# Modulation computed as rows with the weights streamed, and loads in another order, in an AdaLN block on one core

## The reference

```python
mod = (_silu(L0_c) @ L0_wmod).reshape(2, 6, 1, 512)      # L0_c (2, 512), L0_wmod (512, 3072)
sa, ca, ga, sb, cb, gb = (mod[:, 0], ..., mod[:, 5])
ga = (2 * (ga >= 0) - 1) * jnp.maximum(jnp.abs(ga), 0.25)   # gb likewise
h = _layernorm(x) * (1 + ca) + sa
x = x + ga * attn(h)      # projection 512x512, rotation of 64 features, relu, tanh, group norm,
                          # then swapaxes and reshape (tokens and channels change places)
h = _layernorm(x) * (1 + cb) + sb
x = x + gb * ffn(h)       # gate, up (512 -> 1376), silu(gate) * up, down; each weight is lut[idx],
                          # a table of 16 values looked up by an int32 index matrix
```

## Time and profile before

| | us |
|---|---|
| median of 3 runs | 1061.77 (1061.48 to 1063.47) |
| the profiled execution: its time | 1063.87 |
| the profiled execution: its span | 1061.6 |
| start, to the first projection | 0 to 46.48 |
| block 0 | 46.48 to 89.75 (43.27) |
| block 1 | 89.75 to 131.02 (41.27) |
| block 2 | 131.02 to 184.04 (53.02) |
| block 3 | 184.04 to 221.26 (37.22) |
| bridge, to the first feed-forward matmul | 221.26 to 266.13 (44.87) |
| the rest | 266.13 to 1061.6 |

### The profile page before, as it was taken

How to read it: one execution, slowest core, us unless ns; L and a number is a source line. 1 busy time by engine, 2 the same in 40 slices (tenths; PEclk the granted TensorE clock), 3 DMA queues, 4 the chain that set the end, 5 groups by cost and what they waited for, 6 DMA issues and landing times.

```text
span 1061.6 us, 13109 instructions
## 1 busy us (share of the span) xinstructions
PE 960.3 (90%) x4480; PEld 464.8 (44%) x4480; DVE 603.0 (57%) x1384; ACT 410.0 (39%) x621; POOL 185.2 (17%) x156
## 2 busy tenths in 40 slices
PE   5869669977888988999899999999999999999998
PEld 5534326433333433444444444444444444444443
DVE  5599995997589874334887876322222432222312
ACT  2365854566554633224543532332222421222200
POOL 3111202036456540112202200110000101000000
PEclk9989887988899999999999999999999999999999
DMA  8667363531001021234235114222000112000011
GB/s 291 214 178 218 68 185 64 178 100 40 20 20 30 20 80 50 80 110 119 40 119 158 32 48 159 80 70 89 0 0 0 55 44 102 0 0 0 1 40 40
DMA packets 33740, 83.40 MB, mean 79 GB/s; under 512 B 2977, under 2 KB 2977, under 8 KB 30625
## 3 DMA queue, kind: packets, MB, share of 16 engines
q1 hardware_dynamic: 32544, 74.47, 21.4%
q0 software_dynamic: 1152, 8.39, 4.3%
HBM read 63.98 MB, written 18.87 MB: 78 GB/s over the span
## 4 chain that ended last, share of the span: by engine, by line
PE 68%; DVE 17%; issue 6%; ACT 5%; DMA 1%; SPq 1%; POOL 1%; DVEq 0%; ACTq 0%; POOLq 0%
PE ps L1163 27%; PE ps L1197 22%; PE ps L1130 7%; PE ps L1152 4%; DVE hid L834 3%; PE ps L1118 2%; DVE R L856 2%; PE ps L1175 2%; PE ps L1210 2%; DMA w_all<-wmod_dram 1%; DVE hd L865 1%; ACT R L571 1%; DVE st L750 1%; ACT w_all L562 1%; PE ps L1142 1%
## 5 line engine op out<-in xcount | busy, mean ns | idle before, releaser
L1163 PE MATMUL ps<-h,w_all 128*128 128x512 f16 x1920 | 424.7, 383 | 18.8 <-DVE hd L865 16.3
L1163 PEld LDWEIGHTS ps<-h,w_all 128*128 (+1 forms) x1920 | 188.5, 99 | 252.3 <-issue 19.5
L1197 PE MATMUL ps<-w_all,hid 128*128 128x512 f16 x1056 | 231.1, 381 | 4.7 <-DVE w_all L1047 4.7
L1197 PEld LDWEIGHTS ps<-w_all,hid 128*128 128x128 f16 x1056 | 103.6, 98 | 129.5 <-DVE w_all L1047 5.2
L865 DVE SCALAR_TENSOR_TENSOR hd<-ps,col,sg 128x512 f32<-128x512 f32 x80 | 59.9, 748 | 149.5 <-ACT sg L532 149.5
L532 ACT ACTIVATE sg<-ps,col 128x512 f32<-128x512 f32 x80 | 54.6, 682 | 181.8 <-PE ps L1163 181.1
L890 DVE SCALAR_TENSOR_TENSOR hd<-ps,col,gbB 128x512 f32<-128x512 f32 x32 | 24.0, 751 | 148.4 <-PE ps L1197 148.1
L1152 PE MATMUL ps<-hid,w_all 128*128 128x512 f16 x352 | 90.1, 419 | 12.9 <-DVE hid L834 12.9
L547 ACT ACTIVATE hid<-hd 128x512 f16<-128x512 f32 (+1 forms) x88 | 55.0, 628 | 113.0 <-DVE hd L865 99.7
L1130 PE MATMUL ps<-WQ,work 128*128 128x512 f16 x384 | 89.1, 394 | 4.0 <-DVE col L980 3.1
L427 POOL TENSOR_TENSOR h<-h,h 128x512 f16<-128x512 f32 x32 | 37.3, 1186 | 306.5 <-ACT h L517 306.5
(11 more groups left out here) (112 smaller groups left out, 840.6 us busy)
## 6 DMA issues: line engine op xcount, KB each, us to landing
R<-x_dram SPq DMA_DIRECT2D x16, 1024.0 KB, 6.9
xa<-x_dram SPq DMA_DIRECT2D x14, 1024.0 KB, 6.2
hid<-idx_dram SPq DMA_DIRECT2D x44, 256.0 KB, 6.9
R<-bias_dram POOLq DMA_DIRECT2D x8, 1024.0 KB, 8.4
out_dram<-R SPq DMA_DIRECT2D x32, 256.0 KB, 2.2
x_dram<-R SPq DMA_DIRECT2D x7, 1024.0 KB, 5.0
w_all<-wmod_dram SPq DMA_DIRECT2D x6, 1024.0 KB, 15.2
h<-idx_dram SPq DMA_DIRECT2D x11, 256.0 KB, 2.6
```

Of the source, the lines that this page charges most:

```text
L1163: ins = nc.tensor.matmul(bank(GU[2 * s + t]), W[wp][:, bass.ds(at, P)], h2[hp][:, s, k], start=(k == 0 and i == 0), stop=(k == K - 1 and i ...
L1197: ins = nc.tensor.matmul(bank(QY[par]), hid[hp][:, bass.ds(at, P)], W[wp][:, w_at:w_at + BLK], start=(j == 0 and i == 0), stop=(j == J - 1 ...
```

## The change

Each section is now one product of 4 matmuls: `cT`, widened to 32 columns (the two batches repeated 16 times), is stationary, and 512 columns of weights stream past. The result is a tile of 32 rows at partitions 0, 32 or 64 of one PSUM bank (`mod_product`). ScalarE copies it to SBUF (`copy_mod`). `mod_vec` then turns rows into vectors by transposes of 2x128 pieces, four for each section; `mod_row` repeats a row over all partitions by one matmul for each batch, with a column of the identity broadcast. The gate is made once on the 32 rows (`gate_rows`), and VectorE only copies the repeated rows out. GA's vectors and rows are made after block 0's projection, and those of SB, CB and GB in block 3 and the bridge. The loop of TensorE over blocks now covers 1 and 2.

```diff
             load_mod(SA)
+            load_x(x_toks[0, 0], 0)
+            load_mod(CA)
             sp.dma_start(wq_f32, wq.rearrange("(k p) n -> p k n", p=P)).then_inc(wq_in, 16)
-            load_mod(CA)
-            load_x(x_toks[0, 0], 0)
             load_idx(0, 0)
-            load_idx(1, 1)
             load_mod(GA)
...
-            load_rows(0, rows_of_block(0, 0))
-            for s in (SB, CB, GB):
-                load_mod(s)
+            load_idx(1, 1)
+            load_x(x_toks[0, 1], 1)
             for w in range(2, AHEAD):
                 load_idx(w, w % 2)
+            load_rows(0, rows_of_block(0, 0))
...
+                if q == 0:
+                    load_idx(AHEAD, 0)
+                    store_bias(0)
+                for w in range(AHEAD * (q + 1) + (q == 0), AHEAD * (q + 2) - last):
                     load_idx(w, w % 2)
+                if q == 0:
+                    for s in (SB, CB, GB):
+                        load_mod(s)
...
+            def copy_mod(n, sections):
+                act.wait_ge(mod_mm, n + 1)
+                for i in (s % 3 for s in sections):
+                    ins = nc.scalar.activation(mod_rows[i], bank(QY[1])[32 * i:32 * (i + 1)], ACT.Copy)
+                ins.then_inc(mod_copied, 1)
+
+            copy_mod(0, (SA, CA))
+            norm(0)
             act.wait_ge(lut_split, 1)
             half_idx(0, 0)
+            act.wait_ge(vec_ready, 1)
+            affine(0, CA, SA, 0, hq[0], lambda: None, halves=(0,))
+            copy_mod(1, (GA,))
+            affine(0, CA, SA, 0, hq[0], lambda: None, halves=(1,))
             half_idx(1, 1)
-            norm(0)
-            act.wait_ge(vec_ready, 1)
-            affine(0, CA, SA, 0, hq[0], lambda: None)
-            act.wait_ge(row_ready, 1)
-            make_bias(0)
...
+                if q == 0:
+                    tanh(q, 3)
+                    act.wait_ge(row_ready, 1)
+                    make_bias(0)
                 if not last:
                     norm(q + 1)
-                tanh(q, 3)
+                if q:
+                    tanh(q, 3)
...
+                    copy_mod(2, (SB, CB, GB))
...
+            stats(0)
             dve.wait_ge(wq_in, 16)
             magnitude(wq_s, wq_f32)
             v.tensor_reduce(c_wqmax, wq_s, axis=AX, op=ALU.max).then_inc(wq_max, 1)
-            stats(0)
...
+            def gate_rows(n):
+
+                dve.wait_ge(mod_copied, n + 1)
+                m = mod_rows[GA]
+                gate_of(m, m, mod_rows[SA], mod_rows[CA]).then_inc(gate_made, 1)
...
-                step(gate_of(flat(vec[:, GA]), flat(gate_ps[:, GA]), gs[:, 3, 0:K * BATCH],
-                             gs[:, 3, K * BATCH:2 * K * BATCH]))
+                v.tensor_copy(vec[:, GA], gate_ps[:, GA])
                 for b in range(BATCH):
                     dve.wait_ge(row_mm, b + 1)
-                    step(gate_of(gaB[:, b], bank(GU[b]), hd[:, 0], hd[:, 1]))
-                    ins = v.memset(col[:, 14:15], 0.0)
+                    ins = v.tensor_copy(gaB[:, b], bank(GU[b]))
                 ins.then_inc(row_ready, 1)
             masks(0, 0)
-            gates_of_attn()
+            gate_rows(1)
...
+                if q == 0:
+                    rope_relu(q, q, 3)
+                    gates_of_attn()
                 if not last:
                     stats(q + 1)
-                rope_relu(q, q, 3)
+                if q:
+                    rope_relu(q, q, 3)
...
-                if q == NB - 2:
-                    scales_of_ffn()
...
             stats(LN_B[0], xa, 1)
+            scales_of_ffn()
+            gate_rows(2)
...
-                step(gate_of(gbB[:, b], bank(QY[b]), hd[:, 0], hd[:, 1]))
+                ins = v.tensor_copy(gbB[:, b], bank(QY[b]))
+            step(ins)
...
+            def mod_product(sections):
+
                 for s in sections:
+                    i = s % 3
                     pe.wait_ge(mod_in[s], 16)
+                    for k in range(K):
+                        ins = nc.tensor.matmul(bank(QY[1])[32 * i:32 * (i + 1)],
+                                               cT[:, k],
+                                               mod_w[s][:, k], start=k == 0, stop=k == K - 1)
+                ins.then_inc(mod_mm, 1)
...
+                        ins = nc.tensor.transpose(bank(to)[:, at:at + BATCH],
+                                                  mod_rows[s % 3][0:BATCH, kb * P:(kb + 1) * P],
+                                                  ident[0:BATCH, 0:BATCH])
...
-            mod_vec((SA, CA))
-            mod_vec((GA,), GU[3])
-            transpose_x(0, 0)
-            mod_row(GA, GU)
+            mod_product((SA, CA))
+            mod_vec(0, (SA, CA))
+            pe.wait_ge(vec_ready, 1)
+            transpose_x(0, 0, halves=(0,))
+            mod_product((GA,))
+            transpose_x(0, 0, halves=(1,))
             pe.wait_ge(wq_ready, 1)
             pe.wait_ge(diag_ready, 1)
+            pe.wait_ge(mod_copied, 2)
...
                 project(q, q, 0)
+                if gates:
+                    pe.wait_ge(gate_made, 1)
+                    mod_vec(1, (GA,), GU[3])
+                    mod_row(GA, GU)
+                    pe.wait_ge(row_ready, 1)
...
                 if last:
-                    mod_row(GB, QY)
+                    pe.wait_ge(q_taken, A * NB)
+                    mod_product((SB, CB, GB))
                     transpose_g(q, q)
...
-                if scales:
-                    mod_vec((SB, CB))
+                if last:
+                    mod_vec(2, (SB, CB))
...
+            pe.wait_ge(vec_ready, 2)
+            mod_row(GB, QY)
             for i in range(3, 6):
                 sum_chunk(w + i, i % 2)
```

More of the change, by code:

```diff
@@ L316, in _ @@
                     load_early_rows()
-                for w in range(AHEAD * (q + 1), AHEAD * (q + 2) - last):
+                if q == 0:
+                    load_idx(AHEAD, 0)
+                    store_bias(0)
+                for w in range(AHEAD * (q + 1) + (q == 0), AHEAD * (q + 2) - last):
                     load_idx(w, w % 2)
+                if q == 0:
+                    for s in (SB, CB, GB):
+                        load_mod(s)
                 if not last:
@@ L1207, in mod_vec @@
+            def mod_vec(n, sections, to=QY[1]):
+                pe.wait_ge(mod_copied, n + 1)
+                for s in sections:
                     for kb in range(K):
                         at = (s * K + kb) * BATCH
-                        for k in range(K):
-                            ins = nc.tensor.matmul(bank(to)[:, at:at + BATCH], mod_w[s][:, k, kb * P:(kb + 1) * P],
-                                                   cT[:, k], start=k == 0, stop=k == K - 1)
+                        ins = nc.tensor.transpose(bank(to)[:, at:at + BATCH],
+                                                  mod_rows[s % 3][0:BATCH, kb * P:(kb + 1) * P],
+                                                  ident[0:BATCH, 0:BATCH])
@@ L1212, in mod_vec @@
                 ins.then_inc(vec_mm, 1)
             def mod_row(s, banks):
-                if banks is QY:
-                    pe.wait_ge(q_taken, A * NB)
-                pe.wait_ge(mod_in[s], 16)
+                pe.wait_ge(gate_made, s // 3 + 1)
                 for b in range(BATCH):
-                    for k in range(K):
-                        ins = nc.tensor.matmul(bank(banks[b]), cT[:, k, b:b + 1].broadcast_to((P, P)),
-                                               mod_w[s][:, k], start=k == 0, stop=k == K - 1)
-                    ins.then_inc(row_mm, 1)
+                    nc.tensor.matmul(bank(banks[b]), ident[0:BATCH, b:b + 1].broadcast_to((BATCH, P)),
+                                     mod_rows[s % 3][0:BATCH], start=True, stop=True) \
+                      .then_inc(row_mm, 1)
@@ L1234, in attn_block @@
+            def attn_block(q, last=False, gates=False):
                 w = AHEAD * q
                 project(q, q, 0)
+                if gates:
[3 more added lines that the diff above has]
+                    pe.wait_ge(row_ready, 1)
                 sum_chunk(w, 0, True)
@@ L1248, in attn_block @@
                     transpose_g(q, q + 1)
-            pe.wait_ge(row_ready, 1)
-            with pe.Fori(0, NB - 2) as q:
+            attn_block(0, gates=True)
+            with pe.Fori(1, NB - 1) as q:
                 attn_block(q)
-            attn_block(NB - 2, scales=True)
-            pe.wait_ge(vec_ready, 2)
             attn_block(NB - 1, last=True)
```

24 lines of the change are left out of this document (10 added, 14 removed).

## The result

| | median us | lowest to highest | runs |
|---|---|---|---|
| before | 1062.0 | 1061.5 to 1066.2 | 10 |
| after | 1056.2 | 1053.5 to 1059.9 | 10 |

The ratio is 0.9942, with an interval from 0.9924 to 0.9959: 5.8 us faster, where 14.4 were forecast. The profiled execution of after took 1054.04 (span 1051.8), that of before 1063.87 (span 1061.6).

A forecast was written before the change was run, and what follows sets the result against it. Start bound by the modulation chain, blocks 0 and 1 by VectorE, block 2 lengthened by `mod_vec` and a slow `sum_chunk`. -11.0 + 1.6 + 5.4 - 11.7 + 0.5 + 0.8 = -14.4, from 1061.8 to 1047.4; range 1041.0 to 1054.0.

The forecast's parts named there:

- Start, 1.1 too much: Start: reordered loads and streamed products bring the first projection from 46.48 to 35.5, a gain of 11.0.
- Rival (c): Start: GpSimd's 5.74 of issue begins only with the maximum, low halves near 33, projection 39.0; +3.5, 1050.9; chance 0.13.
- Block 0, right: Block 0: gate copies behind the fourth `rope_relu` add 1.6 on VectorE, which bounds the block.
- Block 1, 3 too little: Block 1: SB, CB and GB queued ahead of block 2's tokens make VectorE's statistics wait, +5.4, at most 6.4.
- Block 2, right: Block 2: loses `mod_vec` and the slow `sum_chunk`, becoming 41.27 instead of 53.02, -11.7.
- Block 3, 1.2 too little gain: Block 3: three-section product takes 10.5 against `mod_row`'s 7.03, partly regained in the second transposes; +0.5, between 0 and 1.2.
- Bridge, 1.7 too little: Bridge: scales and `gate_rows` delay VectorE by 2.5, mostly covered; +0.8, between 0 and 2.9.
- so this is covered there: Bridge: VectorE's added 2.5 hides in its 5.72 idle for GpSimd's index conversion; if not, it costs the 2.5.
- (a): Block 1: the three megabytes are hidden and there is no wait; 1042.0; chance 0.20.
- (b): Start: streamed products do not bring TensorE's clock up; gain 5.2 instead of 11.0, 1053.2; chance 0.12.
- (d): Start and block 3: products using only 32 output columns sink TensorE to 1.2 GHz; slower, +3.2, 1065.0; chance 0.04.
- (e): Start: reordering does nothing because something else holds the projection near 46; 1058 to 1061; chance 0.03.

The follow-up runs named there:

- each alone: After with GA's product moved behind the second transposes of block 0: 1055.2 us; or after with the maximum across partitions left out: 1053.3 us.
- both 2.9: After with GA's product behind the second transposes and the maximum across partitions left out too: projection at 33.67, 1051.2 us, ratio 0.9872.

## Why the prediction was wrong

Most mechanisms were named rightly, and no rival came out whole. But two covers were assumed that were not there, two sizes were off, and so was the choice of base. The forecast missed by 8.8: 4.6 in the stages, 4.0 in the base, 0.2 in the median of before itself.

- **Start, 1.1 too much.** Loads, products, norm and transposes came as worked out. The step that failed is "the low half at 34.98 started at once after ScalarE, with no such gap": that row had 11.65 of idle ahead of it, which hid GpSimd's way back from its library. Rival (c) had two halves. The first fell, because the 5.93 ended 1.5 after the maximum, not 5.7 later. The second held: 7.29 of issue ahead of the low halves. The low halves began at 30.04, and the projection came 1.1 later than forecast, not 3.5. How much of the 1.1 is this gap's is not shown apart from the other chain, GA's product (5.31 instead of 4.7) with the transposes behind it: without the reduction the projection still began at 36.32. The Trainium skill ("GPSIMD Engine Reference", 2.1 Instruction dispatch) gives about 6 us for the first call, without the wait for an event; 5.93 agrees in size. The time that the prediction took from that rule did not come, since the gap began ahead of the maximum.
- **Block 0, right:** +1.5.
- **Block 1, 3 too little.** The wait was foreseen with its place and cause, and its bound of 6.4 was exceeded. The step that failed is the bound itself, which added three megabytes at 2.7 to 2.8, 8.1, to the old landing; the tokens landed 9.5 later. 3.8 of that is their later issue, as SP's own issues stood still (4.02 and 2.68, elsewhere 0.39 and 0.67), and 5.7 the longer way to landing; the accumulating transfer stretched beside them from 8.5 to 13.4. And the 1.0 taken off the bound for idle slices was not there. VectorE was busy 39.01, as before (39.06): nothing but waiting was added. The block grew by 0.5 more than the wait; the transposes that ran slow behind it (0.9 longer) may be that, which is not shown. Without the three loads the block is 41.4.
- **Block 2, right:** 41.29.
- **Block 3, 1.2 too little gain.** The term "24 records at 0.44, 10.5" was mis-sized: they took 7.11, since the sections overlap at their borders. The second transposes took 1.31 instead of 1.97, as worked out.
- **Bridge, 1.7 too little.** The step that failed is "so this is covered there". The wait for GpSimd stayed at 5.46, as the prediction itself listed among the signs of being right, but that shows that nothing was covered, since GpSimd is late with VectorE: the masks delay the sum (219.17), behind it stand the transposes on TensorE (224.04), then ScalarE's affine steps, and for these GpSimd waits before its low halves and the conversion. And the sum behind the longer idle fell to the slow level (5.03 instead of 3.63).
- **The base, 4.0.** "The differences are inside the span, so I take them from the median" took the profile of before as a fair stand-in. It was 1.8 above its median; the profile of after was 2.2 below its own. In these ten executions the median of before is nearly its floor (1061.5 to 1062; later sets gave medians of 1063.0 to 1063.5), while after's spread over 6.4 us. A forecast for the median of after would have needed a term for that spread, which one profile cannot give.

Of the rivals, (a) is what the kernel becomes with the three loads moved: 1047.6 measured where it said 1042.0, short by the same base, bridge and start. (b) and (d) fell: the 32-column products rose to records of 0.43 in the start, and ran at that in block 3. (e) fell with the start's 9.9.

## What to carry to other kernels

Where the next wait is a transfer, loads of later use go behind it in the queue, even if the total fits: three megabytes cost 8.2 us in one place and, sixteen us later, 0.1 in that block and at most 0.7 in the next. A row that "starts at once" shows no hidden cost only if the engine's idle before it is shorter than that cost. Before a stage is priced from the trace, ask which of two chains ends there and how far the second is behind: each alone gave 0.5 or less here, both 2.9. And compare more than one profile of a stage: the same start ended at 36.1 once and at 38.6 once.

## What the runs showed of the hardware that I had not expected

- GpSimd stands still twice around a cross-partition reduction: 5.7 to 6.8 us ahead of it, begun without waiting for its input, and 6.6 to 7.5 us ahead of the next ordinary operation where nothing else covers it. Both are "issue" in nearly all traces, they vary by a microsecond between executions, and both are gone where the reduction is left out. What it does in them no trace shows.
- float32 matmuls of 32 output columns that go to different partition groups of one bank overlap: 24 records took 10.5 by count, 7.11 section by section and 3.63 interleaved.
- GpSimd and VectorE instructions took longer side by side. Two low halves on GpSimd mostly take 2.3 to 2.6 us, and took 3.1 to 5.5 at places beside VectorE's work; eight mask instructions (L854) take 2.75, and in the starts took 3.7 to 6.6 beside GpSimd's. Often one of the two paid and not both; what decides it was not tried.
- TensorE kept 2.4 GHz (0.22 per matmul) after 2.41 and 2.50 us of idle, and was at 1.2 GHz at first after 3.55, 4.20 and 4.99. But before's transposes ran at the slow level after 2.25 too, so the last gap alone does not decide it.
